# Mamba-style layer and LoRA feed-forward on one core: the scan kept channel-major, two heads per pass of the array, projections run between its steps

## The reference

```
x = x + mixer(layernorm(x));  x = x + lora_ffn(layernorm(x))
mixer: proj = x @ in_w.T -> gate (8192), xBC (8192 + 2*8*128), dt (128 heads)
  xBC = silu(causal conv of 4 taps + bias);  xBC -> xs (128 heads x 64), B, C (8 groups x 128)
  dt = softplus(dt + bias);  cum = cumsum(dt * A) inside a chunk
  y_intra[i] = sum_j<=i (C_i.B_j) * exp(cum_i - cum_j) * dt_j * x_j        (per head)
  y_inter[i] = exp(cum_i) * C_i . state;   state = exp(cum_last)*state + sum_j B_j*dt_j*exp(cum_last-cum_j)*x_j
  y = y_intra + y_inter + D*x;  g = y * silu(gate);  g = g / rms(g over the group's 1024 channels) * norm_w
  out = g @ out_w.T
lora_ffn: silu(L1(x)) * L3(x) -> L2, with L(x) = x @ w.T + 2 * (x @ a.T) @ b.T, 1376 hidden
```

## Time and profile before

| | |
|---|---|
| median of 3 runs | 1972.45 us (1969.2 to 1976.3) |
| profiled execution, span from first to last instruction | 1972.3 us |
| median less that span | 0.15 us |
| TensorE busy | 1920.5 us, 97% |
| VectorE busy | 1349.0 us, 68% |
| ScalarE busy | 1160.2 us, 59% |
| GpSimd busy | 599.1 us, 30% |
| mean granted TensorE clock | 0.988 |

### The profile page before, as it was taken

The page is one execution under the profiler, slowest core; times in us unless marked ns, Lnnn a source line. Parts: engine busy times, 40 slices in busy tenths (PEclk is TensorE's granted clock), DMA queues, the critical chain, the costliest instruction groups (busy, mean ns, idle before and its releaser), DMA issues. The chain is left out here.

```text
span 1972.3 us, 30097 instructions
## 1 busy us (share of the span) xinstructions
PE 1920.5 (97%) x9642; PEld 1562.7 (79%) x9642; DVE 1349.0 (68%) x2342; ACT 1160.2 (59%) x2132; POOL 599.1 (30%) x553
## 2 busy tenths in 40 slices
PE   7789999999999999999999999999999999999999
PEld 5578887888878887888878878878788888877777
DVE  6787757776876768776777677776877688853112
ACT  5756665665766666666566565667666666642121
POOL 4431145112721163114411271116311452232221
PEclk9899999999999999999899999999999999999999
DMA  4321141214121222214121412122221421131101
GB/s 145 107 83 54 54 135 56 60 49 141 50 66 56 90 87 67 65 43 141 51 65 44 141 51 65 48 88 96 67 65 43 137 70 47 58 104 43 30 1 43
DMA packets 89940, 143.23 MB, mean 73 GB/s; under 512 B 20656, under 2 KB 23104, under 8 KB 89760
## 3 DMA queue, kind: packets, MB, share of 16 engines
q1 hardware_dynamic: 89760, 141.04, 23.2%
HBM read 136.28 MB, written 4.72 MB: 71 GB/s over the span
## 5 line engine op out<-in xcount | busy, mean ns | idle before, releaser
L1134 DVE SCALAR_TENSOR_TENSOR xdt<-bank,par,xdt 128x509 f32<-128x509 f32 (+2 forms) x480 | 326.4, 741 | 77.1 <-ACT xdt L736 75.9
L1237 PE MATMUL bank<-x_h,wx_h 128*128 128x512 f32 x648 | 257.0, 397 | 10.9 <-DVE xdt L1134 6.2
L574 POOL TENSOR_TENSOR skip<-skip,d_row 128x1024 f32<-128x1024 f32 x64 | 121.8, 1903 | 479.9 <-ACT skip L752 479.9
L1238 PE MATMUL bank<-x_l,wx_h 128*128 128x512 f32 x648 | 254.6, 393 | 0.0
L1323 PE MATMUL bank<-xdt,decay 128*128 128x64 f32 x2048 | 243.8, 279 | 10.8 <-issue 10.8
L1239 PE MATMUL bank<-x_h,wx_l 128*128 128x512 f32 x648 | 254.2, 392 | 0.0
L1323 PEld LDWEIGHTS bank<-xdt,decay 128*128 128x128 f32 x2048 | 241.8, 197 | 14.2 <-issue 13.3
L767 ACT ACTIVATE decay<-decay,cols 128x128 f32<-128x128 f32 x448 | 150.4, 396 | 124.1 <-DMA decay<-cum_scratch 122.5
L1237 PE MATMUL bank<-ow_h,gT_h 128*128 128x512 f32 x512 | 222.2, 434 | 0.0
L1237 PE MATMUL bank<-wg_h,x_h 128*128 128x512 f32 x512 | 207.4, 405 | 0.0
L1239 PE MATMUL bank<-wg_h,x_l 128*128 128x512 f32 x512 | 201.1, 393 | 0.0
(11 more groups left out here) (176 smaller groups left out, 3871.2 us busy)
## 6 DMA issues: line engine op xcount, KB each, us to landing
decay<-cum_scratch SPq DMA_DIRECT2D x256, 256.0 KB, 3.5
raw<-in_wx SPq DMA_DIRECT2D x80, 256.0 KB, 2.8
raw<-in_w SPq DMA_DIRECT2D x52, 256.0 KB, 2.8
skip<-in_w SPq DMA_DIRECT2D x32, 256.0 KB, 4.2
xw<-in_w SPq DMA_DIRECT2D x18, 256.0 KB, 4.5
state<-in_w SPq DMA_DIRECT2D x16, 256.0 KB, 2.7
sg<-in_w SPq DMA_DIRECT2D x16, 256.0 KB, 5.4
y<-in_w SPq DMA_DIRECT2D x16, 256.0 KB, 5.6
```

The source lines that it names most:

```text
L574: pool.tensor_tensor(s, s, spread(d_row[:, :], HDIM), ALU.mult).then_inc(skip_ready, 1)
L1134: dve.scalar_tensor_tensor(out=conv[:, n % 4, s:], in0=conv_bank[n % 4][:, 0:SEQ - s], scalar=w, in1=conv[:, n % 4, s:], op0=ALU.mult, op1 ...
L1237: pe.matmul(dst, wh, xh, start=(k == 0), stop=False)
L1238: pe.matmul(dst, wh, xl, start=False, stop=False)
```

## The change

A group is cut into two **units**, one batch each. While the four chunks of a unit are scanned, the 18 tiles (10 conv, 8 gate) of the next unit are projected, 5, 4, 5 and 4 in the four steps. Each tile is loaded for each unit, so 36 projection tiles and 8 output tiles a group go through the split, with room for three split projection tiles. The four raw buffers are shared. The scan's result stays channel-major: xdt (64 columns a head) is the stationary operand and decay the moving one, and two heads write partitions 0 to 63 and 64 to 127 of one bank. `turn_g`, the scaling and the adding of `across` go. In their place exp(cum), broadcast to all partitions by four DMAs (`ce`), is multiplied by C on VectorE, and its product with the state accumulates in the same bank. The gate is projected channel-major too. The causal mask is laid on the decay by GpSimd (affine_select filling with 1e38), which leaves one exp with bias for each head on ScalarE in place of `gaps` and the exp of four heads. The sum of squares over the partitions is made by GpSimd adds and a matmul with a column of ones. GpSimd also makes xw and the low part of g. The low part of the output weights goes to VectorE. The feed-forward has buffers of its own; its first product comes behind the last norm transpose. 

```diff
+SLOT_TILES = [[("g", 0), ("c", 0), ("c", 1), ("c", 2), ("c", 3)],
+              [("g", 1), ("c", 4), ("c", 5), ("c", 6)],
+              [("g", 2), ("c", 7), ("c", 8), ("c", 9), ("g", 3)],
+              [("g", 4), ("g", 5), ("g", 6), ("g", 7)]]
+WRING = 3
+RAW = 4
```

On SyncE:

```diff
+            def body(g, last):
+                for k in range(CHUNKS):
...
+                        load_par(gu, bu)
+                        load_unit(gu, bu)
...
+                        for q in range(QUARTERS):
+                            sp.wait_ge(in_done, (g * CHUNKS + k) * QUARTERS + q + 1)
+                            load_decay(gn, kn, q)
+                            if kn % SC > 0:
+                                load_ce(gn, kn, q)
...
+                    for j in range(at, ends):
+                        body_refill(g, j, last)
```

On GpSimd, with the mask:

```diff
+                    for i in tiles[:2]:
+                        w_low("p", g, b, i)
...
+                    if more:
+                        mask(gn, kn)
+                    gT_low(g, k)
+                    for i in tiles[2:3]:
+                        w_low("p", g, b, i)
+                    square_sum(g, k)
+                    for i in tiles[3:]:
+                        w_low("p", g, b, i)
+                    if more:
+                        skip_of(gn, kn)
+                    inverse_root(g, k)
+                    if more:
+                        weigh_x(gn, kn)
...
+                    pool.affine_select(out=d, in_=d, compare_op=ALU.is_ge, fill=fill, base=0,
+                                       pattern=[[0, QH], [1, P]], channel_multiplier=-1).then_inc(mask_ready, 1)
```

On ScalarE, in one step (`drain` is the first tap of a conv tile, or the silu of a gate tile), with the exps behind it:

```diff
+                    if c > 0 and not ffn:
+                        drain(gu, bu, FIRST_TILE[c] - 1)
+                    for i in tiles[:1]:
+                        w_high("p", g, b, i)
+                    if c > 0 and not ffn:
+                        silu_of(FIRST_TILE[c] - 1)
+                    for i in tiles[1:2]:
+                        w_high("p", g, b, i)
+                    outs(2)
+                    for i in tiles[:1]:
+                        drain(gu, bu, i)
...
+                    gT_high(g, k)
+                    outs(2)
+                    for i in tiles[2:3]:
+                        w_high("p", g, b, i)
+                    if more:
+                        copy_b(gn, kn)
+                        exps(gn, kn, 0)
+                    for i in tiles[1:2]:
+                        if conv_of(i) is not None:
+                            drain(gu, bu, i)
+                    square(g, k)
+                    if more:
+                        for q in range(1, QUARTERS):
+                            exps(gn, kn, q)
+                    outs(2)
+                    for i in tiles[1:2]:
+                        if conv_of(i) is None:
+                            drain(gu, bu, i)
+                        silu_of(i)
+                    for i in tiles[3:4]:
+                        w_high("p", g, b, i)
+                    outs(2)
+                    for n, i in enumerate(tiles[2:-1]):
+                        drain(gu, bu, i)
+                        for j in tiles[4 + n:5 + n]:
+                            w_high("p", g, b, j)
+                        silu_of(i)
...
+                for h in range(q * QH, (q + 1) * QH):
+                    last = act.activation(decay[:, h, :], decay[:, h, :], ACT.Exp, bias=cols[:, b, CUM, c, h:h + 1], scale=-1.0)
```

On VectorE, with the product for the state behind it:

```diff
+                    taps_of(before)
+                    outs(2)
+                    sum_y(g, k)
+                    gated(g, k)
+                    if more:
+                        scale_x(gn, kn)
+                        copy_cb(gn, kn)
...
+                    taps_of(tiles[:1])
+                    outs(2)
+                    fade(g, k)
...
+                    if more:
+                        scores(gn, kn, 0)
+                    taps_of(tiles[1:2])
+                    outs(2)
+                    add_state(g, k)
...
+                        for q in range(QUARTERS):
+                            across(gn, kn, q)
+                        scores(gn, kn, 1)
+                        scores(gn, kn, 2)
+                    taps_of(tiles[2:3])
+                    outs(2)
+                    if more:
+                        scores(gn, kn, 3)
+                    taps_of(tiles[3:-1])
+                    accumulate(g, k)
...
+                d = ce[:, quarter(q), :]
+                dve.tensor_tensor(d, d, bcT[:, b, 1, tok(c)].unsqueeze(1).broadcast_to([P, QH, P]), ALU.mult).then_inc(ce_ready, 1)
```

On TensorE, inside the loop of `inside` over pairs of heads, and then the step:

```diff
+                    for a in range(2):
+                        h = 2 * n + a
+                        last = pe.matmul(dst[a], xdt[:, h * HDIM:(h + 1) * HDIM], decay[:, h, :], start=True, stop=(c == 0))
+                    if c > 0:
+                        for a in range(2):
+                            h = 2 * n + a
+                            last = pe.matmul(dst[a], state[:, h * HDIM:(h + 1) * HDIM], ce[:, h, :], start=False, stop=True)
...
+                    inside(g, k)
+                    for i in tiles[:1]:
+                        project(gu, bu, i)
+                    if more:
+                        turn_x(gn, kn)
+                        match(gn, kn)
+                    for i in tiles[1:2]:
+                        project(gu, bu, i)
+                    new_state(g, k)
+                    for i in tiles[2:3]:
+                        project(gu, bu, i)
...
+                    out_half(g, k, 0)
+                    for i in tiles[3:4]:
+                        project(gu, bu, i)
+                    square_total(g, k, more)
+                    out_half(g, k, 1)
+                    for i in tiles[4:]:
+                        project(gu, bu, i)
```

1623 lines of the change are left out of this document (797 added, 826 removed).

## The result

The changed kernel takes 2413.16 us, the median of four runs (2404.41 to 2417.11), against 1974.18 us for the kernel before, run beside it: a ratio of 1.2235, 95% interval 1.2199 to 1.2271. Slower was right; the time lies 273 us above the forecast of 2140 and 103 us above the range.

A forecast was written before the change was run, and what follows sets the result against it. TensorE bounds the kernel before; late just-in-time weights were to put holes in its list. 120 before the first inside + 48 last half + 235 tail + 7.5 groups of 231.7 (218.5 + 5.2 + 8.0) = 2141, said 2140; range 1940 to 2310.

The forecast's parts named there:

- rival 2: Inside on TensorE: column halves don't run beside each other, 23.8 us more a group, 2320 us; chance 0.12.
- Four other parts hide or nearly do: Scan step: decay and exp(cum) loads, SP's refills, the cdec load and VectorE's list add nothing or nearly nothing.
- with a ring of four to cover it: SP's queue: refills stand behind the decay loads and wait for w_low, covered by four raw buffers.
- the tail: Behind the last inside: 229 us before, less 8.3 of TensorE's work, plus 12 bared and a slow start: 235.
- The group's first step: k = 0: eight ow copies on ScalarE, five in the chain's way, 31.1 us; ring could add 5; boundary 5.2.
- some 15 us: Last half-group's steps without tiles: chain turn_x, scale_x, copy_b, exps, scores, 15 us each; 48 in all.
- Contention: GpSimd and VectorE hold each other up: 0 to 2.6 us a step, taken as 1.0, 8.0 a group.
- The clock: TensorE after idles: some eight matmuls at 1.2 GHz, 0 to 1.6 us a step, taken as 0.
- Rival 3: As forecast, but TensorE's clock falls in every step: group 244.5 us, time 2237; chance 0.10.
- Rival 1: TensorE stays the bound, tile 3's weights aren't late, kernel faster: group 192 us, time 1843; chance 0.15.
- floor for TensorE's list: TensorE's own work in a group: 187.0 us, or 192 with the boundary.
- the 2.6 us a group that the prediction bounded and left out: TensorE: array drain at changes of tiling mode, twice a step, at most 2.6 us a group, counted as nothing.

The follow-up runs named there:

- f2_sp: Changed kernel with SyncE's order alone altered: decays, refills behind the first two tiles, ce loads, other refills; two output-weight refills moved into k = 0: 2316.7 us.
- e1_cdec: Changed kernel with cdec loaded in 128 pieces of 256 bytes in place of 2048 of 16: 2371.8 us.
- e3: Changed kernel with the third and fourth tile's weights made earlier on ScalarE and GpSimd: 2297.7 us.
- b1: b0 with output weights later in the ring, output product later in a group's first step, and output ahead of the fourth tile in a unit's last: 2032.9 us.
- b0: Changed kernel with e1_cdec, e3 and f2_sp joined, and ScalarE's copy of the second tile ahead of the silu that waits for taps: 2084.0 us.
- b3: b2 with the second tile's w_low back in its own step, taps ahead of scores, k = 0 reordered, last norm behind masks and scores: 1990.5 us.
- a1_across: Changed kernel with VectorE multiplying only one head's first 16 columns of each quarter of ce by C: 2414.5 us.
- b2: b1 with weights of the next step's first two tiles made at this step's end, and smaller moves: 2105.5 us.
- a3_across: b2 with the same cut of VectorE's ce products as a1_across: 1946.4 us.
- f1_clk: Changed kernel with 16 filler products of 512 columns on TensorE ahead of the third tile's wait for weights: 2399.2 us.
- b5: b3 with a unit's third-step tiles swapped, k = 0 moves, and the skip term on ScalarE in place of GpSimd: 1961.8 us against 1971.2 before the change.
- e2: Changed kernel with only the third tile's weights made earlier on ScalarE and GpSimd: 2420.2 us.
- f3: Changed kernel with e3 and f2_sp together: 2207.2 us.
- s1: b2 with inside taking four products of even heads, then four of odd ones, per quarter, in place of taking turns: 2127.6 us.

## Why the prediction was wrong

**The direction and the mechanism held.** Just-in-time weights put holes in TensorE's list: 101 waits for `w_l`, 305.8 us. Inside is 3.5 us, so rival 2 (halves one after the other) fell; the first inside is at 120.9 for 120. The forecast's steps are real: with SyncE's order put right, f2_sp's k = 1 is 27.4 against 27.3, k = 2 30.6 against 30.0.

**The step that failed** is the part "Four other parts hide or nearly do". It took the decay's 3.5 us from the earlier trace rows, in a kernel whose DMAs moved 143 MB in all where the new one moves 231 (the page's DMA line), and had SyncE's refills stand behind the loads "with a ring of four to cover it". Neither held with eight DMAs a step ahead of the refills: decays landed in 5.2 us, masks waited 243.5 us for them, and a refill issued at T + 3 stopped ScalarE in k = 1 for 5.89 us right ahead of `copy_b`, so that `copy_b` ended at T + 11.5 in place of T + 5.45. f2_sp prices SyncE's order at 96 us. The prediction read each engine's list of what is queued behind a waiting instruction, but not the two lists into which a late DMA feeds: the third tile's weights (tile 2 in the prediction's count) stand ahead of `copy_b` on ScalarE, and behind the masks on GpSimd. The same part put the cdec load at no more than a delay of the first step's decay and gave it no term; e1_cdec prices it at 41 us.

If the two add, for which there is no run without e3's order, they are 137 of the 273 us, and the tail is 34. The rest, about 100, is by the table for the most part some 5 us in k = 0 and 2 each in k = 3 and k = 7 of a group. It is the part that stays open, as no run takes it apart; b1's order, with the output ahead of the fourth tile, has k = 3 at 22.0.

**The group's first step** was given 31.1 + 5.2, with 5 more for the ring "kept for the range". It took 49.1. e1_cdec takes 5.1 off it, e3_w23 7.3, and from b0 to b1 3.5 go with the later output weights and output product. These overlap: with e3's order the cdec load shows in k = 7 and no longer in k = 0.

**The tail** was 317 in place of 283: the three steps without tiles took 23 to 24.5 us each, not 15. In each, TensorE waits 4.06 us for `gT_l`, until T + 10.8 in the first and T + 12.8 in the others: `gT_l` follows ScalarE's `gT_high`, which stands behind the copies of the late norm, and the norm goes through VectorE, GpSimd, TensorE and ScalarE in turn. Behind it comes the output product, which the chain of "some 15 us" leaves out. b3, which puts the norm behind masks and scores, has 21.5 to 22.5.

**Contention**, 1.0 a step, was priced for a kernel in which it cost nothing: the products that were cut are worth nothing in the changed one (a1_across) and 159 us in b2 (a3_across). So far as a1_across tells, the 60 us that the sum held for it (8.0 a group) were not needed, and the other terms fell short by that much more. The scores' mean of 1071 ns lies in the 0.7 to 1.2 forecast. Two of GpSimd's prices were off: a mask is 0.63 us undisturbed, not 1.0, and `xw`, for which no row stood behind the 1.4, is 1.9.

**The clock** at nothing was right within 14 us net (f1_clk). The slow stretch was longer than the eight matmuls assumed: behind the 4.55 us wait in k = 1 fourteen stand 0.43 apart, and the slowed work still ends ahead of the wait for the fourth tile. It cost next to nothing, although TensorE's busy time a group rose: in the stretch 379 to 2093 us, 6.5 groups, TensorE is busy 1401.09 us, 215.5 a group, where its list was reckoned at 187, at a granted clock of 0.90. Here slow work ahead of a wait was free. Rival 3, 12.8 us a group for the clock, fell by the same run, in which the group is 1.8 shorter.

**Rival 1** (TensorE bound, 1843) did not come true, but its floor for TensorE's list was right. In a3_across, steps without a wait take 23.7, 26.5, 21.9 and 24.8, 193.8 a group against the 192 reckoned. But with 317 + 121 around it, even that floor gives 438 + 7.5 x 194 = 1893, and no order tried reached it: b5 is at G = 202.7.

What stays open: what the engines wait for in the pause at the group's start that the cdec load lengthens; how b5's loss in k = 0 splits between VectorE's list and the ring; and what part of a3_across's gain is waiting between VectorE and GpSimd and what is VectorE's own load, beyond the estimate above.

## What to carry to other kernels

When work is made just in time, follow each tile from its DMA's issue on, through every queue with what now stands ahead of it in each, and take a landing time from a queue as full as the new one, not from the old trace. A wait that an edit removes says nothing about the next: e2 alone gave nothing, and in f3, b0 and b1 the same edit was part of 206 to 380 us; and contention that costs nothing in a starved kernel can cost much when it is fed (0 and 159 us for one edit). A slow clock in the records of an engine that waits is a symptom until a filler run shows a price.

## What the runs showed of the hardware

- A load of 32 KB in 2048 pieces of 16 bytes made the next two DMA issues take 3.20 and 2.53 us in place of 0.33, landed in 12.1 us in place of 3.0, and cost 41 us in all for sixteen loads (changed kernel, e1_cdec).
- Products of 64 stationary columns in alternating column halves cost 0.218 us a pair (two heads, two records each); in runs of four of one half, inside is a third longer (4.80 against 3.64, s1 and b2).
- At the change from full-width products to these and back, starts stand 0.33 and 0.31 us apart (from 953.35 to 953.68 and from 957.01 to 957.32 in the changed kernel), against 0.23 inside a tile. If there is a drain, it is of some 0.1 us each; the 2.6 us a group that the prediction bounded and left out would not have mattered.
- Sixteen filler products ahead of the third tile of a step raised the mean granted clock from 0.903 to 0.947 and moved the time by 0.6%.
- GpSimd's affine_select over 128x512 takes 0.63 to 0.64 us undisturbed, below the 1.0 taken; its mean in the changed kernel is 0.81.
- VectorE's product of 128x512 with both inputs in SBUF takes 0.64 us where GpSimd is idle and up to 2.04 beside it; its taps, with one input in PSUM, take 2.31 for three beside GpSimd's work (b1, 1050.59) and without it (b2, 880.10) alike.
